# Recommendation tower in float32: six pairs of products a chunk in two parts instead of four, four low parts by VectorE, first transfers and last stage rearranged

## The chip, the core and the metric

The kernel runs on one core of a Trainium2 chip. The metric is the device time of one launch in microseconds (us); lower is better. Engines: TensorE (PE, its weight loads PEld), VectorE (DVE), ScalarE (ACT), GpSimd (POOL), SyncE (SP, which only issues transfers here).

## What is computed

For 512 rows, 32 embeddings of 16 numbers are gathered from 32 tables. Three cross layers follow, each a big matrix product over all products of two fields; then a small dense network.

```python
x0 = h = e                                  # (512, 32, 16)
for i in range(3):
    z = (x0[:, :, None, :] * h[:, None, :, :]).reshape(B, F * G, E)
    y = relu(einsum('oc,bce->boe', Ws[i], z) + bs[i][None, :, None])
    x_keep, h = (y[:, :64], y[:, 64:]) if i != 2 else (y, y)
    xs.append(x_keep)
z = sum(concatenate(xs, axis=1), axis=2)    # (512, 256)
h = maximum(concatenate([z, dense_ctx], 1) @ W_top1 + b_top1, 0)
h = maximum(h @ W_top2 + b_top2, 0)
y = h @ W_top3                              # (512, 1)
```

## The kernel before

**Chunks and steps.** The batch is cut into 16 chunks of 32 rows; a chunk has 32 x 16 = 512 columns. A *step* (layer, chunk, k) makes one group of four product tiles z (128x2048) and multiplies them. Layer 0 has one step a chunk, layers 1 and 2 have four each (k = 0 to 3). A step's four tiles are two *pairs*, i = 0 and 1. The order of steps is a written table. From chunk c = 2 on it repeats, and I number the nine steps of a round s0 to s8:

| s0 | s1 | s2 | s3 | s4 | s5 | s6 | s7 | s8 |
|---|---|---|---|---|---|---|---|---|
| (1,c,0) | (2,c-1,0) | (1,c,1) | (2,c-1,1) | (0,c+1,0) | (1,c,2) | (1,c,3) | (2,c-1,2) | (2,c-1,3) |

**Who does what.** VectorE makes the products z of a step: L414 for layers 1 and 2 (one operand h in PSUM, the other x_pair in SBUF), L402 for layer 0 (both operands in SBUF), and L426 for the squares of layer 0. A pair is multiplied in one of two ways. *Unsplit* (L605): two float32 matmuls, each of which the trace records as two. *Split* (L618): ScalarE rounds z to a high part z_high (L498), another engine subtracts it to get z_low (L362 on GpSimd), and TensorE does six matmuls of the fast rounded type: high by high, high by low weight, low by high weight. The layer 0 split has one more small matmul (L623).

**Order on the engines.** Every engine works through its own list in order. TensorE does at place n of the table first the unsplit pairs of step n and then the split pairs of step n-2 (`BEHIND`). ScalarE does at place n first the layer outputs that are due there (`OUTPUTS`), then the high parts of step n. A layer output (`layer_out`, L512) waits until the last pair of its layer and chunk in TensorE's order (`CLOSES`) is done; then it writes relu of the bank twice, 64 rows each, as h (the input of the next layer's products) and once as kept. The output of (1,c) stands at s8 and that of (0,c+1) at s0 of the next round, in this order. The products of s0 need h of layer 0 (h1), those of s1 need h of layer 1 (h2). Five z slots and four z_high/z_low slots are used in turn.

Before the change, the split pairs of a chunk from 1 on are both pairs of layer 0 and i = 1 of (1,k=0), (1,k=1), (2,k=1) and (2,k=2): six of eighteen, all their low parts on GpSimd. So (1,c) is closed by an unsplit pair of s6.

**Transfers.** GpSimd gathers the embeddings (L349, eight a chunk, three chunks ahead). SyncE stores them to a scratch buffer in DRAM (`store_x`) and loads them back repeated over partitions: `load_x0` (x_rep, x_rot for layer 0, 1.25 MB a chunk) and `load_pair` (x_pair for layers 1 and 2, 4 MB a chunk). At the start TensorE does BUSY = 56 transposes (L658) until the first chunk has arrived.

**Last stage.** The first dense layer's sums go through relu with the bias into hid1, then are rounded and split (L581, L584, L465), and a second dense layer (L628) and the last row (L689, L691) follow.

Of the kernel before, what the change touches and what calls it, by code (L numbers as in the profile page):

```python
# [6 lines left out]
P = 128  # L7
# [3 lines left out]
CHUNKS = BATCH // ROWS  # L11
# [7 lines left out]

Z_SLOTS, PAIR_SLOTS, X_SLOTS = 5, 4, 4  # L20
X0_LOADS, SMALL, TOPS = GROUP + 1, 2, COPIES + 2
BUSY = 56
# [45 lines left out]
FIRST = ([(1, 0, k) for k in range(GROUPS)] + [(2, 0, 0), (0, 1, 0)] + [(2, 0, k) for k in range(1, GROUPS)]  # L68
# [49 lines left out]
def behind():  # L118

    due = {n: [] for n in range(len(PLAN))}  # L120
    for n, step in enumerate(PLAN):
        for pair in step.by("vector", "pool"):
            due[min(n + 2, len(PLAN) - 1)].append(pair)
    return due


BEHIND = behind()
# [17 lines left out]
def dlrm_tower(nc, idx_in, row0_in, ident_in, sel_in, signs_in, columns_in, table, dense, w0_in, w12_in, w_top1, w_top2, out):  # L145
    with ExitStack() as ctx:  # L146
# [6 lines left out]
        def sem(name):  # L153
# [7 lines left out]
        rows_all = sb("rows_all", [P, CHUNKS * GATHERS], I32)  # L161
# [21 lines left out]
        columns = sb("columns", [P, 11])  # L183
        bias, bt1, bt2, wt3 = columns[:, 0:3], columns[:, 3:7], columns[:, 7:9], columns[:, 9:11]
# [23 lines left out]
        hid1 = x_pair[:, 0, 0:4, :]  # L208
# [42 lines left out]
        top1_done, hid1_made, hid1_rounded, hid1_ready = (sem("top1_done"), sem("hid1_made"), sem("hid1_rounded"),  # L251
                                                          sem("hid1_ready"))
# [44 lines left out]
        def _(sp):  # L297
# [37 lines left out]
            tops = [(wd[EMBED * i:EMBED * (i + 1)], w_top1[2 * P:, :]) for i in range(COPIES)] + [  # L335
                (wt1, w_top1[0:2 * P, :].rearrange("(k p) n -> p k n", p=P)),
# [5 lines left out]
            sp.dma_start(out.rearrange("b o -> o b"), result[:]).then_inc(out_stored, 16)  # L342
# [405 lines left out]
```

## Time and profile before

| | |
|---|---|
| median of 3 runs | 548.99 us (548.51 to 549.04) |
| the profiled execution's own time | 548.4 us |
| its span, first to last instruction | 546.6 us |
| TensorE busy | 505.7 us, 93% |
| VectorE busy | 376.5 us, 69% |
| GpSimd busy | 364.1 us, 67% |
| ScalarE busy | 198.8 us, 36% |
| mean granted TensorE clock | 0.978 |

The span is 1.8 us shorter than the execution's own time, which is 0.6 us below the median. A busy share is a mean over stages; which engine sets the time in a round has to be read from the order of events in that round.

### The profile page before, as it was taken

The page shows a single profiled execution, that of the slowest core. Times are in us where ns is not written, and L with a number is a line of the kernel's source. Part 1 is how long each engine was busy: PE and PEld are TensorE (multiplying, and loading weights), DVE is VectorE, ACT ScalarE, POOL GpSimd, SP SyncE. Part 2 cuts the span into 40 slices and gives each one's busy share as a digit, 9 for nine tenths or more (in the row PEclk, how much of TensorE's full clock was granted, in tenths as well). Part 3 has the DMA queues.
Part 4 walks back from the last instruction along what each step waited for, and adds up shares of the span by engine and source line. Part 5 has one row for each costly group of instructions (what it writes and reads, how often), then busy time and mean ns, then how long its engine had stood idle before and what let it go on. Part 6 is the DMA issues. An engine that isn't in the chain of part 4 may idle for free.

```text
span 546.6 us, 4327 instructions
## 1 busy us (share of the span) xinstructions
PE 505.7 (93%) x1474; PEld 277.4 (51%) x1474; DVE 376.5 (69%) x216; ACT 198.8 (36%) x257; POOL 364.1 (67%) x222
## 2 busy tenths in 40 slices
PE   0977947899999999999999999999999989899988
PEld 0733414455555555565555555555555554455555
DVE  1274526595959595959688695959595968967743
ACT  1212132433444443424342434434443525241244
POOL 5770527497969788796969696969697754715050
PEclk9988887899999999999999999999999999999999
DMA  7697989349997979797878787979789777451200
GB/s 229 144 201 204 210 221 196 100 98 252 222 251 170 255 159 254 158 227 166 230 164 226 172 215 165 225 167 244 164 197 222 171 190 161 90 110 11 74 0 0
DMA packets 33591, 94.49 MB, mean 173 GB/s; under 512 B 7889, under 2 KB 15057, under 8 KB 25122
## 3 DMA queue, kind: packets, MB, share of 16 engines
q1 hardware_dynamic: 27090, 90.82, 69.5%
q10 hardware_dynamic: 2384, 2.35, 2.0%
q0 software_dynamic: 4096, 1.06, 1.6%
q8 instruction: 11, 0.18, 0.1%
q14 instruction: 10, 0.08, 0.1%
HBM read 92.04 MB, written 2.10 MB: 172 GB/s over the span
## 4 chain that ended last, share of the span: by engine, by line
PE 73%; DMA 8%; DVE 7%; issue 4%; POOL 3%; SPq 2%; ACT 1%; POOLq 1%; DVEq 0%; ACTq 0%
PE acc L605 26%; PE acc L618 14%; PE spare L605 12%; PE x_bank L605 11%; DMA x_scratch<-gathered 4%; DVE z L414 4%; PE x_bank L618 3%; PE spare L618 3%; POOL gathered L349 3%; DMA gathered<-in_table,rows_all 2%; DMA x_rot<-x_scratch 1%; SPq L276 1%; POOLq L146 1%; DVE zl_parts L426 1%; PE acc L628 1%
## 5 line engine op out<-in xcount | busy, mean ns | idle before, releaser
L362 POOL TENSOR_TENSOR z_low<-z,z_high 128x1024 fp32r<-128x1024 f32 x90 | 221.4, 2472 | 130.1 <-ACT z_high L498 129.4
L414 DVE TENSOR_TENSOR z<-h,x_pair 128x2048 f32<-128x2048 f32 (+1 forms) x65 | 144.8, 2249 | 106.1 <-ACT h L512 104.6
L605 PE MATMUL acc<-z,w_direct 128*128 128x512 f32 x384 | 176.3, 603 | 15.2 <-DVE z L414 15.2
L349 POOL DMA_INDIRECT gathered<-in_table,rows_all x128 | 142.5, 1113 | 33.4 <-issue 27.1
L498 ACT ACTIVATE z_high<-z 128x1024 fp32r<-128x1024 f32 x90 | 93.3, 1054 | 145.1 <-DVE z L414 124.9
L605 PEld LDWEIGHTS acc<-z,w_direct 128*128 128x128 f32 x384 | 73.6, 193 | 95.7 <-issue 72.6
L605 PE MATMUL spare<-z,w_direct 128*128 128x512 f32 x200 | 92.4, 603 | 4.5 <-DVE z L414 4.5
L605 PE MATMUL x_bank<-z,w_direct 128*128 128x512 f32 x200 | 92.5, 608 | 3.9 <-DVE z L414 3.9
L414 DVE TENSOR_TENSOR z<-h_odd,x_pair 128x2048 f32<-128x2048 f32 x32 | 72.2, 2278 | 8.4 <-ACT h_odd L512 8.4
L414 DVE TENSOR_TENSOR z<-h_even,x_pair 128x2048 f32<-128x2048 f32 x32 | 72.2, 2279 | 7.9 <-ACT h_even L512 7.9
L605 PEld LDWEIGHTS spare<-z,w_direct 128*128 128x128 f32 x200 | 38.4, 193 | 47.9 <-issue 43.0
L605 PEld LDWEIGHTS x_bank<-z,w_direct 128*128 128x128 f32 x200 | 38.9, 195 | 45.0 <-issue 43.2
L618 PE MATMUL acc<-z_high,w_high 128*128 128x512 f32 x124 | 57.5, 544 | 1.6 <-POOL z_low L362 1.6
L402 DVE TENSOR_TENSOR z<-x_rep,x_rot 128x2048 f32<-128x2048 f32 x15 | 44.2, 2944 | 7.8 <-DMA x_rot<-x_scratch 7.8
L618 PE MATMUL acc<-z_high,w_low 128*128 128x512 f32 x124 | 38.8, 395 | 0.0
L618 PE MATMUL acc<-z_low,w_high 128*128 128x512 f32 x124 | 38.3, 391 | 0.0
L618 PEld LDWEIGHTS acc<-z_high,w_high 128*128 128x128 f32 x124 | 23.6, 191 | 25.6 <-issue 22.4
L512 ACT ACTIVATE h<-acc,columns 64x512 f32<-64x512 f32 x32 | 20.9, 652 | 39.5 <-PE acc L618 35.2
L512 ACT ACTIVATE kept<-acc,columns 64x512 f32<-64x512 f32 (+1 forms) x32 | 21.9, 683 | 30.4 <-PE acc L618 29.8
L618 PEld LDWEIGHTS acc<-z_low,w_high 128*128 128x128 f32 x124 | 23.3, 188 | 5.4
L618 PEld LDWEIGHTS acc<-z_high,w_low 128*128 128x128 f32 x124 | 23.3, 188 | 5.2
L431 DVE TENSOR_REDUCE sum<-kept 128x32 f32<-128x512 f32 x32 | 21.6, 676 | 5.9 <-ACT kept L512 5.9
(140 smaller groups left out, 266.4 us busy)
## 6 DMA issues: line engine op xcount, KB each, us to landing
x_pair<-x_scratch SPq DMA_DIRECT2D x124, 512.0 KB, 7.3
x_rot<-x_scratch SPq DMA_DIRECT2D x60, 256.0 KB
x_rep<-x_scratch SPq DMA_DIRECT2D x15, 256.0 KB
w_direct<-in_W SPq DMA_DIRECT2D x2, 1024.0 KB, 8.5
gathered<-in_table,rows_all POOLq DMA_INDIRECT x128, 7.1
x_scratch<-gathered SPq DMA_DIRECT2D x32, 64.0 KB, 1.6
x_pair<-x_scratch ACTq DMA_DIRECT2D x4, 512.0 KB, 16.5
x_pair<-in_W_top SPq DMA_DIRECT2D x2, 512.0 KB, 4.7
```

The lines of the kernel that those rows point to most:

```text
L146: with ExitStack() as ctx:
L276: eng.dma_start(x_pair[HALF * a:HALF * (a + 1), c % 2, GROUP * k:GROUP * (k + 1), :], rows.unsqueeze(0).to_broadcast([HALF, GROUP, N])).th ...
L349: pool.indirect_dma_start(gathered[:, c % X_SLOTS, j, :], None, table, bass.IndirectOffsetOnAxis(ap=rows.bitcast(U32), axis=0),).then_inc( ...
L362: nc.gpsimd.tensor_tensor(z_low[:, slot_of(pair)], products_of(pair), z_high[:, slot_of(pair)].bitcast(F32), ALU.subtract).then_inc(low_po ...
L402: nc.vector.tensor_tensor(z[:, step.group % Z_SLOTS], x_rep[:].unsqueeze(1).to_broadcast([P, GROUP, N]), x_rot[:], ALU.mult).then_inc(z_ma ...
L414: nc.vector.tensor_tensor(z[:, step.group % Z_SLOTS, first:end], h[:].unsqueeze(1).to_broadcast([P, end - first, N]), x_pair[:, chunk % 2, ...
L426: nc.vector.scalar_tensor_tensor(out=zl_parts[:], in0=zl_high[:].bitcast(F32), scalar=signs[:, 0:1], in1=zl_full[:], op0=ALU.mult, op1=ALU ...
L431: nc.vector.tensor_reduce(total[:, chunk * ROWS:(chunk + 1) * ROWS], kept.rearrange("p (b e) -> p b e", b=ROWS), AX.X, ALU.add).then_inc(m ...
L498: nc.scalar.activation(z_high[:, slot_of(pair)], products_of(pair), ACT.Copy).then_inc(high_made, 1)
L512: return nc.scalar.activation(dst, bank[rows, :], ACT.Relu, bias=bias[rows, layer:layer + 1])
L605: op = nc.tensor.matmul(bank_of(pair)[:], w_direct[:, first + i], products_of(pair)[:, i], start=i == 0 and pair is OPENS[pair.layer, pair ...
L618: op = nc.tensor.matmul(bank_of(pair)[:], w[:, at + i], zs[:, slot, i], start=part == i == 0 and pair is OPENS[pair.layer, pair.chunk], st ...
```

## The change

It has four parts. (1) `SPLIT` gets two more entries, (1,2,1) and (2,0,1): eight of a chunk's eighteen pairs are split. (2) Four of the low parts, (0,0,1), (1,2,1), (2,0,1) and (2,1,1), and all of layer 2 in the last chunk, go to VectorE, one place behind their products (`LOWS`). (3) The first transfers are issued in another order, the steps (2,0,1) and (0,1,0) change places, the products of (2,0,0) come in two halves, and BUSY is 28. (4) In the last stage the bias of the first dense layer is a row of the dense matmul, so one ScalarE operation makes the rounded hid1 straight from the bank, VectorE makes its low part from the bank, and TensorE begins each k with the four matmuls that need only the high part.

```diff
-BUSY = 56
+BUSY = 28
-FIRST = ([(1, 0, k) for k in range(GROUPS)] + [(2, 0, 0), (0, 1, 0)] + [(2, 0, k) for k in range(1, GROUPS)]
+FIRST = ([(1, 0, k) for k in range(GROUPS)] + [(2, 0, 0), (2, 0, 1), (0, 1, 0), (2, 0, 2), (2, 0, 3)]
-SPLIT = ((1, 0, 1), (1, 1, 1), (2, 1, 1), (2, 2, 1))
+SPLIT = ((1, 0, 1), (1, 1, 1), (1, 2, 1), (2, 0, 1), (2, 1, 1), (2, 2, 1))
+BY_VECTOR = ((0, 0, 1), (1, 2, 1), (2, 0, 1), (2, 1, 1))
 def hands(layer, chunk, k):
-    return tuple("pool" if chunk and (layer, k, i) in AT else "tensor" for i in range(2))
+    def by(of):
+        if not chunk or of not in AT:
+            return "tensor"
+        return "vector" if of in BY_VECTOR or (layer, chunk) == (2, CHUNKS - 1) else "pool"
+
+    return tuple(by((layer, k, i)) for i in range(2))
...
+def lows():
+
+    due = {n: [] for n in range(len(PLAN))}
+    for n, step in enumerate(PLAN):
+        for pair in step.by("vector"):
+            due[min(n + 1, len(PLAN) - 1)].append(pair)
+    return due
...
             sp.wait_ge(x_stored[0], 32)
-            for k in range(GROUPS):
+            for k in range(2):
                 load_half(sp, 0, k, 0)
             store_x(sp, 1)
+            for k in range(2, GROUPS):
+                load_pair(0, k)
             sp.wait_ge(start_done, 1)
             load_x0(sp, 1)
-            for k in range(GROUPS):
+            store_x(sp, 2)
+            for k in range(2):
                 load_pair(1, k)
+            wait_made(sp, STEPS[0, 1, 0])
+            sp.wait_ge(last_made, 2)
+            load_x0(sp, 2)
+            for k in range(2, GROUPS):
+                load_pair(1, k)
...
                 free_slot(step)
                 (products if step.layer else products0)(step)
-                for pair in BEHIND[n]:
-                    if pair.by == "vector":
-                        low_part(pair)
+                for pair in LOWS[n]:
+                    low_part(pair)
...
                 act.wait_ge(top1_done, m + 1)
-                nc.scalar.activation(hid1[:, m, :], top_bank[m][:], ACT.Relu,
-                                     bias=bt1[:, m:m + 1]).then_inc(hid1_made, 1)
-                act.wait_ge(hid1_made, m + 1)
-                nc.scalar.activation(hid1_high[:, m, :], hid1[:, m, :], ACT.Copy).then_inc(hid1_rounded, 1)
+                nc.scalar.activation(hid1_high[:, m, :], top_bank[m][:], ACT.Relu).then_inc(hid1_rounded, 1)
```

`BEHIND`, `OUTPUTS`, the order of the nine steps and the number of slots stay (only the split pairs of (0,1) come one place earlier). How the order changes on three engines is shown at one place each, the middle of the program.

TensorE before, from the split pairs of s4 (which close layer 0 of the next chunk in acc0) to s0 of the next round:

```order
L618 MATMUL acc0<-z_high,w_high 128x512 [waits low_pool]
L618 MATMUL acc0<-z_high,w_high 128x512
L623 MATMUL acc0<-zl_parts,wl_parts 128x512 [waits last_parts]
L618 MATMUL acc0<-z_high,w_low 128x512 x2
L618 MATMUL acc0<-z_low,w_high 128x512 x2
L605 MATMUL x_bank<-z,w_direct 128x512 [waits z_made]
L605 MATMUL x_bank<-z,w_direct 128x512
L605 MATMUL x_bank<-z,w_direct 128x512 [waits z_made]
L605 MATMUL x_bank<-z,w_direct 128x512
```

TensorE now, at the same place (spare is the bank of layer 1):

```order
L645 MATMUL acc0<-z_low,w_high 128x512 x2
L632 MATMUL acc2<-z,w_direct 128x512 [waits z_made]
L632 MATMUL acc2<-z,w_direct 128x512
L645 MATMUL spare<-z_high,w_high 128x512 [waits low_dve]
L645 MATMUL spare<-z_high,w_high 128x512
L645 MATMUL spare<-z_high,w_low 128x512 x2
L645 MATMUL spare<-z_low,w_high 128x512 x2
L632 MATMUL acc2<-z,w_direct 128x512 [waits z_made]
L632 MATMUL acc2<-z,w_direct 128x512
```

Behind the close of layer 0 there now stand the unsplit pair of s7 and then the split pair of s5, which is the last of layer 1: (1,c) closes two pairs after (0,c+1), where it used to close before it.

ScalarE at the end of a round, before (first fence) and now (second): the output of layer 1, then that of layer 0.

```order
L512 ACTIVATE h2_even<-spare,columns 64x512 [waits z_made,direct_used]
L512 ACTIVATE h2_even<-spare,columns 64x512
L512 ACTIVATE kept01<-spare,columns 64x512
L512 ACTIVATE h1<-acc0,columns 64x512 [waits sum01_made,z_made,pairs_used]
```

```order
L542 ACTIVATE h2_even<-spare,columns 64x512 [waits z_made,pairs_used]
L542 ACTIVATE h2_even<-spare,columns 64x512
L542 ACTIVATE kept01<-spare,columns 64x512
L542 ACTIVATE h1<-acc0,columns 64x512 [waits sum01_made,z_made,pairs_used]
```

The order is the same; h2 now waits for a split pair (`pairs_used`), and h1 stands behind it.

VectorE, the products from s2 to s6 before:

```order
L414 TENSOR_TENSOR z<-h1,x_pair 128x2048 [waits xp_here_0_1,direct_used]
L431 TENSOR_REDUCE sum01<-kept01 128x32 [waits kept1_out]
L414 TENSOR_TENSOR z<-h2_odd,x_pair 128x2048 [waits low_pool,direct_used]
L431 TENSOR_REDUCE sum2<-kept2 128x32 [waits kept2_out]
L402 TENSOR_TENSOR z<-x_rep,x_rot 128x2048 [waits x0_here,direct_used]
L426 SCALAR_TENSOR_TENSOR zl_parts<-zl_high,signs,zl_full 128x512 [waits last_high]
L414 TENSOR_TENSOR z<-h1,x_pair 128x2048 [waits xp_here_0_2,low_pool,direct_used]
L414 TENSOR_TENSOR z<-h1,x_pair 128x2048 [waits xp_here_0_3,low_pool,direct_used]
```

and now:

```order
L442 TENSOR_TENSOR z<-h1,x_pair 128x2048 [waits xp_here_0_1,direct_used]
L449 TENSOR_TENSOR z_low<-z,z_high 128x1024 [waits high_made]
L459 TENSOR_REDUCE sum01<-kept01 128x32 [waits kept1_out]
L442 TENSOR_TENSOR z<-h2_odd,x_pair 128x2048 [waits low_pool,direct_used]
L459 TENSOR_REDUCE sum2<-kept2 128x32 [waits kept2_out]
L430 TENSOR_TENSOR z<-x_rep,x_rot 128x2048 [waits x0_here,direct_used]
L449 TENSOR_TENSOR z_low<-z,z_high 128x1024 [waits high_made]
L454 SCALAR_TENSOR_TENSOR zl_parts<-zl_high,signs,zl_full 128x512 [waits last_high]
L442 TENSOR_TENSOR z<-h1,x_pair 128x2048 [waits xp_here_0_2,low_pool,direct_used]
L449 TENSOR_TENSOR z_low<-z,z_high 128x1024 [waits high_made]
L442 TENSOR_TENSOR z<-h1,x_pair 128x2048 [waits xp_here_0_3,low_dve,direct_used]
```

Three low parts (L449) stand ahead of the products of s6, and a fourth right behind them.

## Rows read from the trace of the kernel before

**Rows 1.** The page: span; busy time, share and instructions of each engine.

```profile
span 546.6 us, 4327 instructions
PE 505.7 (93%) x1474; PEld 277.4 (51%) x1474; DVE 376.5 (69%) x216; ACT 198.8 (36%) x257; POOL 364.1 (67%) x222
```

**Rows 2.** The chain that ended last, one round: start us, us, what.

```profile
245.18 6.87 PE acc L605 x16
252.04 1.37 PE acc L618 x6
...
256.85 1.72 PE acc L605 x4
...
271.31 1.85 PE acc L618 x8
274.30 5.15 PE x_bank L605 x12
```

**Rows 3.** Timeline at a round's end: start us, us, engine, line, what [idle before].

```profile
271.35 1.32 ACT L512 ACTIVATE h_odd<-acc,columns 64x512 f32<-64x512 f32 x2 [3.32 <-PE acc L605]
...
272.69 0.68 ACT L512 ACTIVATE kept<-acc,columns 64x512 f32<-64x512 f32 x1
...
274.34 1.32 ACT L512 ACTIVATE h<-acc,columns 64x512 f32<-64x512 f32 x2 [0.97 <-PE acc L618]
...
275.79 2.29 DVE L414 TENSOR_TENSOR z<-h,x_pair 128x2048 f32<-128x2048 f32 x1 [6.65 <-ACT h L512]
```

```profile
274.14 5.31 PE L605 MATMUL x_bank<-z,w_direct 128*128 128x512 f32 x12
```

**Rows 4.** Timeline of the round without gathers, by engine (VectorE, GpSimd, TensorE).

```profile
430.81 0.68 DVE L431 TENSOR_REDUCE sum<-kept 128x32 f32<-128x512 f32 x1
431.40 3.03 DVE L402 TENSOR_TENSOR z<-x_rep,x_rot 128x2048 f32<-128x2048 f32 x1
434.36 2.86 DVE L426 SCALAR_TENSOR_TENSOR zl_parts<-zl_high,signs,zl_full 128x512 fp32r<-128x512 f32 x1
437.15 4.48 DVE L414 TENSOR_TENSOR z<-h,x_pair 128x2048 f32<-128x2048 f32 x2
```

```profile
429.92 11.85 POOL L362 TENSOR_TENSOR z_low<-z,z_high 128x1024 fp32r<-128x1024 f32 x4 [2.67 <-ACT z_high L498]
```

```profile
439.48 3.70 PE L605 MATMUL acc<-z,w_direct 128*128 128x512 f32 x8 [1.66 <-DVE z L414]
```

**Rows 5.** Groups by line and shape: busy us, mean ns | idle before.

```profile
L362 POOL TENSOR_TENSOR z_low<-z,z_high 128x1024 fp32r<-128x1024 f32 x90 | 221.4, 2472 | 130.1 <-ACT z_high L498 129.4
...
L498 ACT ACTIVATE z_high<-z 128x1024 fp32r<-128x1024 f32 x90 | 93.3, 1054 | 145.1 <-DVE z L414 124.9 <-DVE z L402 20.2
...
L465 DVE TENSOR_TENSOR z_low<-x_pair,z_high 128x1024 fp32r<-128x1024 f32 x1 | 1.2, 1207 | 0.0
```

**Rows 6.** TensorE behind a gap: its timeline, then the 2 us window after it (granted clock ahead of the last two figures).

```profile
105.83 5.40 PE L605 MATMUL acc<-z,w_direct 128*128 128x512 f32 x8 [2.14 <-DVE z L414]
```

```profile
106.00:108.00 2.00, 2.00 (x3) 0.81 (x4) 2.00 (x2) 0.00 (x0) 1.70 (x2) 0.53 0.12 16
```

**Rows 7.** Timeline of the head.

```profile
13.93 7.96 PE L658 MATMUL acc<-ident 128*128 128x128 f32 x56
...
80.58 2.29 DVE L402 TENSOR_TENSOR z<-x_rep,x_rot 128x2048 f32<-128x2048 f32 x1 [7.83 <-DMA x_rot<-x_scratch]
...
98.66 2.29 DVE L414 TENSOR_TENSOR z<-h,x_pair 128x2048 f32<-128x2048 f32 x1 [7.94 <-ACT h L512]
```

```profile
85.79 3.59 PE L605 MATMUL acc<-z,w_direct 128*128 128x512 f32 x4 [11.00 <-DVE z L414]
```

**Rows 8.** Timeline of the last chunk and the last stage.

```profile
483.45 2.29 DVE L414 TENSOR_TENSOR z<-h,x_pair 128x2048 f32<-128x2048 f32 x1 [6.43 <-ACT h L512]
...
529.47 0.52 PE L670 MATMUL h<-dense_parts,wd_parts 48*128 48x512 f32 x1
...
536.57 0.47 PE L628 MATMUL acc<-z_high,w_high 128*128 128x512 f32 x1 [0.23 <-DVE z_low L465]
```

More of the change, by code:

```diff
@@ L122, in behind @@
         for pair in step.by("vector", "pool"):
-            due[min(n + 2, len(PLAN) - 1)].append(pair)
+            due[min(n + (1 if (pair.layer, pair.chunk) == (0, 1) else 2), len(PLAN) - 1)].append(pair)
     return due
-BEHIND = behind()
+def lows():
[4 more added lines that the diff above has]
+    return due
+BEHIND, LOWS = behind(), lows()
+HALVED = (STEPS[1, 0, 0], STEPS[2, 0, 0])
 ORDER = list(START.pairs)
@@ L132 @@
 CLOSES = {(pair.layer, pair.chunk): pair for pair in ORDER}
-LAST1 = max((pair for step in PLAN for pair in step.by("pool") if step.layer < 2), key=lambda pair: pair.split)
-LAST_SLOT = max((pair for step in PLAN for pair in step.by("pool") if pair.split % PAIR_SLOTS == PAIR_SLOTS - 1),
+LAST1 = max((pair for step in PLAN for pair in step.by("vector", "pool") if step.layer < 2),
+            key=lambda pair: pair.split)
+LAST_SLOT = max((pair for step in PLAN for pair in step.by("vector", "pool") if pair.split % PAIR_SLOTS == 0),
                 key=lambda pair: pair.split)
@@ L411, in products @@
                 h = h1 if step.layer == 1 else h2[chunk % 2]
-                runs = ((0, 2), (2, 4)) if step is PLAN[0] else ((0, 4),)
+                runs = ((0, 2), (2, 4)) if step in HALVED else ((0, 4),)
                 for first, end in runs:
@@ L543, in _ @@
             act.wait_ge(dense_turned, 1)
-            nc.scalar.activation(dense_high[:], dense_bank[0:COPIES * EMBED, :], ACT.Copy).then_inc(dense_rounded, 1)
+            nc.scalar.activation(dense_high[:], dense_bank[0:COPIES * DENSE, :], ACT.Copy).then_inc(dense_rounded, 1)
             act.wait_ge(x_stored[0], 32)
-            for k in range(GROUPS):
+            for k in range(2):
                 load_half(act, 0, k, 1)
@@ L598, in unsplit @@
                     pe.wait_ge(w12_here[pair.layer - 1], 16)
-                if step is PLAN[0] and pair.i == 0:
-                    pe.wait_ge(first_made, 1)
+                if step in HALVED and pair.i == 0:
+                    pe.wait_ge(first_made, HALVED.index(step) + 1)
                 else:
@@ L679, in _ @@
             for k in range(4):
+                pe.wait_ge(hid1_rounded, k + 1)
+                for m in range(2):
+                    cols = slice(k * 2 * P + m * P, k * 2 * P + (m + 1) * P)
+                    nc.tensor.matmul(acc[m][:], wt2_high[:, cols], hid1_high[:, k, :], start=k == 0, stop=False)
+                    nc.tensor.matmul(acc[m][:], wt2_low[:, cols], hid1_high[:, k, :], start=False, stop=False)
                 pe.wait_ge(hid1_ready, k + 1)
                 for m in range(2):
[L682 to L684 removed]
+                    cols = slice(k * 2 * P + m * P, k * 2 * P + (m + 1) * P)
+                    op = nc.tensor.matmul(acc[m][:], wt2_high[:, cols], hid1_low[:, k, :], start=False, stop=k == 3)
                     if k == 3:
@@ L719 @@
         "table": np.concatenate(tables, axis=0),
-        "dense_ctx": np.asarray(inputs["dense_ctx"]),
+        "dense": np.concatenate([np.asarray(inputs["dense_ctx"]), np.ones((BATCH, 1), np.float32)], axis=1),
     }
```

76 lines of the change are left out of this document (38 added, 38 removed).

## The prediction, written before the changed kernel ran

> **What bounds the kernel now.** I read the page first: TensorE is busy for 505.7 of 546.6 us, VectorE for 376.5 [rows 1]. Then the chain that ended last. From about 110 us to 420 us it is TensorE and nothing else: in [rows 2] the reader sees one of ten equal rounds, from 245.18 to 274.30 us, 29.1 us each. An unsplit pair takes 1.72 us (x4), a split pair 1.37 to 1.39 (x6), and the two pairs of layer 0 with their extra matmul 2.99 (271.31 to 274.30). Twelve unsplit pairs, four split ones and this block give 20.6 + 5.5 + 3.0 = 29.1: no gap is in it.
>
> Then I asked how near the other engines come to ending last, at a round's end and in its middle. At the end [rows 3]: TensorE begins the next work at 274.14, so layer 0 has closed; ScalarE writes h1 from 274.34 for 1.32 us, VectorE starts the products of s0 at 275.79, that is 1.65 us after the close, and needs 2.29. They end at 278.1; TensorE has three pairs meanwhile, 5.15 us, to 279.3, so h1 comes 1.2 us ahead of need. VectorE had waited 6.65 us, but this wait is no free time: it stands behind h1, so whatever is added to VectorE's list ahead of s6 comes after it. So there is a second chain round the loop: close of layer 0, h1, VectorE's products s0 to s6, the two pairs of s6, the split pairs of s4, close of the next layer 0. How little air it has is shown where gathers end and four low parts of GpSimd come in a row [rows 4]: L402 takes 3.03 and L426 2.86 us, because VectorE's operations with both operands in SBUF and GpSimd's subtraction exclude each other (GpSimd's four need 11.85 us, where four of the mean 2.47 of [rows 5] are 9.9). That is 2.1 us more on VectorE, and TensorE stands for 1.66 us at 439.48, at s6.
>
> **The change, part by part.**
>
> *TensorE's work.* Two more split pairs a chunk save 2 x (1.72 - 1.38) = 0.67 us a round: 28.45 us of work instead of 29.12. This would be the gain, if TensorE stayed the bound.
>
> *VectorE's new work.* A low part with 128x1024 elements took 1.21 us on VectorE [rows 5]; starts of successive operations lie 0.08 us closer than their durations, so I take 1.13 each. It needs the high part, 1.06 us on ScalarE [rows 5], which begins 0.1 us after the products. I walk one round from the start of the products of s0 (0), with products 2.20 apart (from 4.48 for two), sums 0.60 (430.81 to 431.40), squares 0.66 (0.74 less the overlap) [rows 4]. Products s1 at 2.20, s2 at 4.40. The low part of s1 could start at 6.60, but its high part stands on ScalarE behind kept of layer 2, which waits for TensorE to close that layer behind s0: 2.33 + 1.72 + 1.38 = 5.43; kept 5.63, high part 6.22 to 7.28; low part 7.32. Sum 8.45, products s3 9.04, sum 11.24, products s4 11.84, low part of s3 14.04, squares 15.17, products s5 15.83, low part of s4 18.03, where GpSimd is still at its own low part of s4 until 18.3, so 0.25 later than free; products s6 19.41, done at 21.69. TensorE by then has done s0 to s5 with gaps of 1.1 us ahead of s3 and 2.3 us ahead of s5 and waits 0.5 us for s6. It then does the pairs of s6 (3.43) and of s4 (2.99).
>
> *The close of layer 1.* In this kernel the split pair of s5 is layer 1's last. TensorE reaches it two pairs after the close of layer 0: 1.72 + 1.38 = 3.10 us later, at 21.73 + 3.43 + 2.99 + 3.10 = 31.25. ScalarE has the output of layer 1 in its list ahead of h1. So h1 waits for a close that it doesn't need: 0.20 to start, 1.34 for h2, 0.68 for kept, 1.32 for h1, 0.13 to VectorE [rows 3] make 3.67. The products of the next s0 start at **34.9**. TensorE has only s8 to cover this, 3.43 us against 3.67 + 2.33, so it stands for 2.5 us there. The new round is 34.9 us against 29.1, +5.8. Without the late close it would be 31.25 - 3.10 + 1.65 = 29.8: the low parts alone cost 0.7 a round, the close 5.1. Queued behind the waiting h1 are all products of the round; behind VectorE's wait for the high part of s1 are s3 to s8.
>
> *Gaps and TensorE's clock.* The walk assumes full clock. In the trace a gap of 2.14 us is followed by a stretch at about half (0.53 granted, the lower level, 1.2 GHz), in which eight matmuls take 5.40 us instead of 3.60: 1.8 us lost [rows 6]. The gap of 1.66 us cost nothing: 3.70 [rows 4]. Shown as the profile shows them (0.15 less than from start to start), the gaps of the walk are 2.35 us ahead of s0 and 2.15 ahead of s5. A loss behind s0 delays the close of layer 2 and so the low part of s1: up to 1.8 a round. A loss behind s5 has 0.5 us of air: up to 1.3. So 0 to 3.1 a round. Both gaps are at or a little above the one that fell, one case only, so I take the middle, 1.5.
> The Trainium skill's page "TensorE: Matmul & The Clock Gate", section "HAM oscillation — how this bites in real kernels", warns of idle gaps longer than any in this walk; by that rule the clock would stay up and nothing be added, and the trace's 2.14 us gap disagrees with it.
>
> *Head.* 28 fewer transposes of 0.142 us [rows 7] start the first chunk 4.0 us earlier; halving the products of (2,0,0) lets TensorE start 1.1 sooner. VectorE's wait of 7.83 us for x_rot ahead of (0,2,0) goes, since this load is now issued one layer 0 step earlier, ahead of two of the four x_pair loads. So TensorE's start at 85.79 [rows 7] comes at 72.9. From there to the products of s0 of chunk 2 there were 12.9 us; now two unsplit pairs, one split and the block, 3.44 + 1.38 + 2.99 = 7.8, a stretch at half clock as now (1.8) and 1.65: 84.1 instead of 98.66, -14.5. Bounds: -4 (only the warm-up) and -18. But layer 1 of chunk 1 then closes 7.9 us after layer 0 and h2 holds up s1 by 5.7 us; with the wait for kept gone (0.7), the first round is 39.9.
>
> *The other rounds.* From s0 of chunk 3 to s0 of chunk 15 there are 12 rounds: 418.8. So s0 of chunk 15 starts at 84.1 + 39.9 + 418.8 = 542.8 (now 483.45 [rows 8]). From there to TensorE's first dense matmul there are 46.0 us (to 529.47). The same walk without a layer 0 step gives 48.0, since the high parts of the last layer 2 pairs wait for the output of chunk 14 and VectorE carries them all; 49 with a half loss of clock.
>
> *Last stage.* 17.1 us from there to the end. TensorE is busy all through it but for 0.23 us at 536.57 [rows 8], which the shorter hand-over removes: -0.3. The removed ScalarE operations (four of 0.7) lie under TensorE's work of the first dense layer.
>
> *Sum.* 542.8 + 49 + 17.1 - 0.3 = 608.6 at full clock, and 13 rounds x 1.5 = 20 for the clock: a span of 628.6, +82 on 546.6. The median lies 2.4 us above the span: **631 us**.
>
> **Rivals.**
> *The clock stays up* in all rounds: 608.6 + 2.4 = 611. For it: the gap of 1.66 that cost nothing, and gaps that are only just longer than the one that did. Against it: that one.
> *The clock falls behind both gaps in every round:* 608.6 + 40 + 2.4 = 651.
> *The other side: h1 isn't held up,* the close of layer 1 coming in time. The place is ScalarE's wait at s8. If the round is 29.8, the 13 rounds give back 66 us of the 82: 608.6 - 66 + 2.4 = 545, and with TensorE as the only bound (28.45 a round) 527. It decides as soon as ScalarE serves h1 within 1.65 us of the close. Against it: the lists of both engines stand fixed, h2 ahead of h1, and the split pair of s5 two pairs after the close. Nothing in the trace lets ScalarE pass a wait.
> *The gather or the loads become late:* a longer round gives them more time; no price.
>
> **How the numbers follow.** Clock falls in part of the gaps: 0.5. Stays up: 0.25. Falls always: 0.18. Not held up: 0.04. Something outside: 0.03. The range goes from a little below the second to the third, with -4 for the head (-18 instead of -14.5): 606 to 652. A difference below 0.2% (1.1 us) can't be told from none here. Slower by more than that holds 0.95; faster 0.04; the same 0.01.
>
> **What would show it.** In the changed profile: rounds of 35 to 38 us in place of 29.1; "DVE z <- ACT h" still the longest wait of VectorE, and TensorE idle <- DVE z in every round, at s0 (2.4 us), s3 (1 us) and s5 (2 us), with VectorE's low part at 1.2 us; ScalarE's h2 starting 0.2 us after a split pair, h1 2.0 us behind it; the granted clock at its lower level in some slices all through the middle; GpSimd's wait for high parts grown. The prediction is wrong if the rounds stay near 29 us, which would mean that h1 is served ahead, or if VectorE's operations are each longer than in these rows.

## The result, and the profile after

The changed kernel took 653.36 us (median of 4 runs, 651.42 to 654.54) against 548.75 us (548.32 to 549.04) for the kernel before on the same chip: a ratio of 1.1925, 95% interval [1.1896, 1.1954]. Predicted were 631 us, 606 to 652. The direction and the mechanism came as forecast; the time lies 22 us above the forecast and 1.4 outside the range. The page of the changed kernel (span, busy time, and in slices TensorE's busy tenths and its granted clock):

```profile
span 651.3 us, 4498 instructions
PE 538.7 (83%) x1506; PEld 296.9 (46%) x1506; DVE 436.6 (67%) x280; ACT 227.1 (35%) x285; POOL 309.1 (47%) x191
PE   1877697978888897888889888888889788889978
PEclk9989997988889998889999888988988898899989
```

Against [rows 1], TensorE is no longer the bound (83%, and part of its busy time is a slower clock), VectorE is 60 us busier, GpSimd 55 us less. The digits 8 of the clock row run all through the middle.

One round, read as [rows 3, 4] were. VectorE (start us, us, what, and idle time before it with what ended it):

```profile
318.93 2.29 DVE L442 TENSOR_TENSOR z<-h,x_pair 128x2048 f32<-128x2048 f32 x1 [7.82 <-ACT h L542]
...
328.04 1.23 DVE L449 TENSOR_TENSOR z_low<-z,z_high 128x1024 fp32r<-128x1024 f32 x1 [2.42 <-ACT z_high L528]
...
334.76 1.22 DVE L449 TENSOR_TENSOR z_low<-z,z_high 128x1024 fp32r<-128x1024 f32 x1
...
338.76 1.21 DVE L449 TENSOR_TENSOR z_low<-z,z_high 128x1024 fp32r<-128x1024 f32 x1
...
356.99 2.29 DVE L442 TENSOR_TENSOR z<-h,x_pair 128x2048 f32<-128x2048 f32 x1 [9.28 <-ACT h L542]
```

ScalarE at this round's end:

```profile
353.50 1.32 ACT L542 ACTIVATE h_even<-spare,columns 64x512 f32<-64x512 f32 x2 [6.90 <-PE spare L645]
354.84 0.68 ACT L542 ACTIVATE kept<-spare,columns 64x512 f32<-64x512 f32 x1
355.54 1.31 ACT L542 ACTIVATE h<-acc,columns 64x512 f32<-64x512 f32 x2
```

TensorE's three gaps in it:

```profile
321.37 2.59 PE L632 MATMUL spare<-z,w_direct 128*128 128x512 f32 x4 [2.54 <-DVE z L442]
...
332.11 1.98 PE L632 MATMUL acc<-z,w_direct 128*128 128x512 f32 x4 [0.95 <-DVE z L442]
...
338.90 3.11 PE L632 MATMUL spare<-z,w_direct 128*128 128x512 f32 x4 [2.06 <-DVE z L442]
```

And windows of 2 us (granted clock ahead of the last two figures), two behind the first gap and one behind the third:

```profile
322.00:324.00 2.00, 2.00 (x5) 0.84 (x4) 2.00 (x2) 0.31 (x1) 1.61 (x1) 0.64 0.23 66
324.00:326.00 2.00, 2.00 (x6) 1.52 (x6) 1.62 (x1) 0.00 (x0) 1.71 (x2) 0.51 0.79 188
...
340.00:342.00 2.00, 2.00 (x4) 0.87 (x3) 2.00 (x1) 0.00 (x0) 1.70 (x2) 0.50 1.05 381
```

The reader sees the chain of the prediction step by step: the output of layer 1 (h_even, at 353.50) ahead of h (355.54), VectorE's products 1.45 us behind that, its whole list behind them, and TensorE idle at s0, s3 and s5. New is how often the clock falls: behind the gap at s0 in every round, behind that at s5 in eight rounds of twelve. The eight rounds with both falls are 38.1 us long and the four with one are 36.7; the mean of the twelve, from s0 of chunk 3 to s0 of chunk 15, is 37.61.

The head on VectorE, for [rows 7], and the first products of chunk 2:

```profile
40.10 2.29 DVE L442 TENSOR_TENSOR z<-h,x_pair 128x2048 f32<-128x2048 f32 x1 [6.08 <-DMA x_pair<-x_scratch]
45.15 2.29 DVE L442 TENSOR_TENSOR z<-h,x_pair 128x2048 f32<-128x2048 f32 x1 [2.76 <-DMA x_pair<-x_scratch]
...
91.67 2.29 DVE L442 TENSOR_TENSOR z<-h,x_pair 128x2048 f32<-128x2048 f32 x1 [2.83 <-ACT h L542]
```

and TensorE's transposes at the start, with the first matmul behind them:

```profile
14.23 5.44 PE L685 MATMUL acc<-ident 128*128 128x128 f32 x28
19.60 1.12 PE L662 MATMUL x_bank<-x_rot 32*128 32x512 f32 x2
```

The last chunk's s0 and the first dense matmul, for [rows 8]:

```profile
582.64 2.29 DVE L442 TENSOR_TENSOR z<-h,x_pair 128x2048 f32<-128x2048 f32 x1 [9.28 <-ACT h L542]
```

```profile
634.27 0.50 PE L697 MATMUL h<-dense_parts,wd_parts 51*128 51x512 f32 x1
```

### The profile page after: what moved, and what is told of

Read it like the earlier page. It is cut to its first block, busy times and chain, and to the rows that moved or that the text cites. A ratio compares the mean times of both kernels' runs of the same rounds, so it can differ in the third digit from the quotient of the medians.

```text
span 651.3 us, 4498 instructions
## 1 busy us (share of the span) xinstructions
PE 538.7 (83%) x1506; PEld 296.9 (46%) x1506; DVE 436.6 (67%) x280; ACT 227.1 (35%) x285; POOL 309.1 (47%) x191
## 4 chain that ended last, share of the span: by engine, by line
PE 49%; DVE 28%; issue 10%; ACT 7%; DMA 3%; POOL 2%; SPq 0%; DVEq 0%; ACTq 0%
DVE z L442 17%; PE acc L632 15%; PE acc L645 13%; PE spare L632 11%; DVE z L430 4%; PE x_bank L645 4%; DVE z_low L449 3%; ACT h L542 3%; DVE sum L459 3%; PE x_bank L632 3%; ACT z_high L528 2%; POOL gathered L377 2%; PE spare L645 2%; DVE zl_parts L454 1%; ACT kept L542 1%
## 5 line engine op out<-in xcount | busy, mean ns | idle before, releaser
L390 POOL TENSOR_TENSOR z_low<-z,z_high 128x1024 fp32r<-128x1024 f32 x59 | 147.9, 2507 | 264.5 <-ACT z_high L528 264.4
L528 ACT ACTIVATE z_high<-z 128x1024 fp32r<-128x1024 f32 x120 | 123.7, 1054 | 200.7 <-DVE z L442 182.8
L377 POOL DMA_INDIRECT gathered<-in_table,row x128 | 161.0, 1258 | 34.9 <-issue 27.5
L632 PEld LDWEIGHTS acc<-z,w_direct 128*128 128x128 f32 x320 | 62.7, 203 | 122.2 <-issue 79.0
L449 DVE TENSOR_TENSOR z_low<-z,z_high 128x1024 fp32r<-128x1024 f32 x61 | 76.2, 1249 | 34.9 <-ACT z_high L528 34.9
L632 PE MATMUL x_bank<-z,w_direct 128*128 128x512 f32 x172 | 79.7, 597 | 11.3 <-DVE z L442 11.3
L645 PE MATMUL acc<-z_high,w_high 128*128 128x512 f32 x156 | 78.2, 584 | 0.0
L442 DVE TENSOR_TENSOR z<-h_even,x_pair 128x2048 f32<-128x2048 f32 (+1 forms) x33 | 72.4, 2216 | 5.3 <-ACT h_even L542 5.3
L645 PE MATMUL acc<-z_high,w_low 128*128 128x512 f32 x156 | 49.9, 401 | 0.0
L542 ACT ACTIVATE h_even<-spare,columns 64x512 f32<-64x512 f32 x16 | 10.4, 652 | 66.7 <-PE spare L645 45.3
```

The source lines that it names most:

```text
L377: pool.indirect_dma_start(gathered[:, c % X_SLOTS, j, :], None, table, bass.IndirectOffsetOnAxis(ap=rows.bitcast(U32), axis=0),).then_inc( ...
L390: nc.gpsimd.tensor_tensor(z_low[:, slot_of(pair)], products_of(pair), z_high[:, slot_of(pair)].bitcast(F32), ALU.subtract).then_inc(low_po ...
L442: nc.vector.tensor_tensor(z[:, step.group % Z_SLOTS, first:end], h[:].unsqueeze(1).to_broadcast([P, end - first, N]), x_pair[:, chunk % 2, ...
L449: nc.vector.tensor_tensor(z_low[:, slot_of(pair)], products_of(pair), z_high[:, slot_of(pair)].bitcast(F32), ALU.subtract).then_inc(low_dv ...
L528: nc.scalar.activation(z_high[:, slot_of(pair)], products_of(pair), ACT.Copy).then_inc(high_made, 1)
L542: return nc.scalar.activation(dst, bank[rows, :], ACT.Relu, bias=bias[rows, layer:layer + 1])
```

## The experiments

A round below is the time from one s0 of VectorE (its products with h of layer 1) to the next. The prediction's walk gave 34.9 us for it at full clock; before it was 29.13 (31.0 in the last two). Diffs are against the changed kernel unless another is named.

### The rounds: what is late, and what the clock costs

**e1, h1 served ahead of h2.** Layer 1's output goes into ScalarE's list one step later.

```
-    at |= {(1, c): PLACE[2, c - 1, GROUPS - 1] if c >= 2 else PLACE[2, c, 0] for c in range(CHUNKS)}
+    at |= {(1, c): PLACE[1, c + 1, 0] if 2 <= c < CHUNKS - 1 else PLACE[2, c - 1, GROUPS - 1] if c >= 2
+           else PLACE[2, c, 0] for c in range(CHUNKS)}
```

> The changed kernel, with ScalarE's output of layer 1 moved behind that of layer 0 (from s8 to s0 of the next round, h1 ahead of h2). Theory (the close of layer 1 holds up h1): s0's products start 1.65 us behind the close of layer 0, not 6.8; the gap ahead of s0 goes. What ends last then is the low part of s1, whose high part stands behind kept of layer 2: walk 32.2 us a round, 33 with the clock falling behind s5. 653 - 13 x (37.6 - 32.2 to 33) = 583 to 594. Rival (VectorE's four low parts are the cost, wherever h1 stands): rounds above 36 us, over 630.

Measured: 596.77 us (one run; the kernel before took 549.16 on this chip), span 595.0, rounds of 32.22 and 33.6 us, 33.16 in the mean. So h2's place ahead of h1 costs 4.45 us a round, and the twelve rounds give back 53 of the 105 us. The time lies 3 us above the expectation: the clock fell behind s5 in eight of the twelve rounds, which makes them 33.6. At full clock the place costs 34.9 less 32.2, 2.7 and not the 5.1 that the prediction had put on it. The timeline of this kernel shows where the rest stays (VectorE's s0, ScalarE's output of layer 2, VectorE's first low part):

```profile
292.89 2.29 DVE L443 TENSOR_TENSOR z<-h,x_pair 128x2048 f32<-128x2048 f32 x1 [4.09 <-ACT h L543]
...
301.08 0.69 ACT L543 ACTIVATE kept<-x_bank,columns 128x512 f32<-128x512 f32 x1 [3.43 <-PE x_bank L646]
...
302.75 1.23 DVE L450 TENSOR_TENSOR z_low<-z,z_high 128x1024 fp32r<-128x1024 f32 x1 [2.26 <-ACT z_high L529]
```

ScalarE writes layer 2's output 8.19 us behind s0 instead of the prediction's 5.63: when h1 comes early, TensorE still has the pairs of s7, s5 and s8 before it (1.72 + 1.38 + 3.43), so it enters s0 later relative to VectorE. The low part of s1, behind that close in ScalarE's list, moves from 7.32 to 9.86, and with it everything behind. What the early h1 gains at one end, the close of layer 2 takes back in part.

**e2, all low parts on GpSimd.**

```
-BY_VECTOR = ((0, 0, 1), (1, 2, 1), (2, 0, 1), (2, 1, 1))
+BY_VECTOR = ()
```

> The changed kernel with all low parts on GpSimd (eight split pairs a chunk as before it); the last chunk's layer 2 stays with VectorE. Theory (late close): h1 is still held up, TensorE's gap of 2.4 us ahead of s0 stays and with it the fall of the clock; 3.67 + 2.33 + 15.5 (TensorE's work s0 to s5) + 6.42 + 3.10 = 31.0 us a round, up to 33 with the clock: 567 to 595. Rival (VectorE's new work is the whole cost): rounds near 29, about 545. Third (GpSimd becomes the bound: eight low parts of 2.5 and eight gathers of 1.25 make 30): idle TensorE waits for z_low, not for z.

Measured: 616.62 us (one run), most rounds of 33.76 or 35.1, mean 34.62: 3.0 less than in the changed kernel, but 22 us above the expectation. The rounds of 33.76 are those in which the clock stayed up; against the 34.93 of e3 below, which is the changed kernel's round at full clock, the four low parts on VectorE cost 1.2 us, and the rest of the 3.0 is the clock's. GpSimd's and TensorE's timeline, at the moment that the split pair of s2 is due:

```profile
316.61 3.05 POOL L377 DMA_INDIRECT gathered<-in_table,row  x1
...
319.68 2.37 POOL L390 TENSOR_TENSOR z_low<-z,z_high 128x1024 fp32r<-128x1024 f32 x1
...
322.11 0.73 PE L645 MATMUL spare<-z_high,w_high 128*128 128x512 f32 x2 [1.86 <-POOL z_low L390]
```

A gather that issues in 0.95 us elsewhere took 3.05 while VectorE worked at its layer 0 products (316.55, both operands in SBUF); the low part behind it comes late, and TensorE now waits for GpSimd where it had waited for VectorE.

The same round shows something on the clock: the gap at s0 is as long as in the changed kernel, and the four matmuls behind it run at full clock (1.96 us where they took 2.59; granted clock 1.00 in the window of 2 us behind it).

```profile
309.00 1.96 PE L632 MATMUL spare<-z,w_direct 128*128 128x512 f32 x4 [2.54 <-DVE z L442]
```

```profile
310.00:312.00 2.00, 2.00 (x9) 1.31 (x8) 2.00 (x2) 0.00 (x0) 1.98 (x1) 1.00 0.00 0
```

**e3, the clock held up.** Fifteen transposes of the identity into a bank that the next pair opens fill TensorE's gaps at s0 and s5. They compute nothing.

```
+                if step.chunk >= 2 and pair.i == 0 and (pair.layer, pair.k) in ((1, 0), (1, 2)):
...
+                    for _ in range(FILL):
+                        nc.tensor.transpose(bank[:, 0:P], ident[:], ident[:])
```

> The changed kernel with 15 transposes of 0.14 us ahead of TensorE's s0 and s5 from chunk 2 on, into banks that are free there (2.1 us of work in gaps of 2.5 and 2.2); nothing else differs. Theory (the gaps cost clock, 2.7 of the 37.6 us a round): granted clock at its upper level in the middle, rounds of 34.9 us, 653 - 35 = 618. Rival (the rounds are longer than the walk for another reason, a queue or the shared port): rounds stay at 37 to 38, 650 or more.

Measured: 624.74 us (one run), 28.6 less than the changed kernel. The page's clock row and TensorE's timeline:

```profile
PEclk9979978999999999999999999999999999999989
```

```profile
309.37 1.80 PE L634 MATMUL spare<-ident 128*128 128x128 f32 x15
311.98 1.98 PE L641 MATMUL spare<-z,w_direct 128*128 128x512 f32 x4 [0.81 <-DVE z L443]
...
325.68 1.80 PE L634 MATMUL acc<-ident 128*128 128x128 f32 x15
327.91 1.98 PE L641 MATMUL spare<-z,w_direct 128*128 128x512 f32 x4 [0.43 <-DVE z L443]
```

The same gaps are there, only filled; the four matmuls behind them take 1.98 us where they took 2.59 and 3.11. Every round in the middle is 34.93 us: the walk, to 0.03. So the walk was right, and 37.61 - 34.93 = 2.7 us a round are the clock's. The twelve rounds give back 32 us; the head was 1.3 and the first round 2.3 longer, in the latter the filling also stands in TensorE's way.

**e6, the late close alone, and e5 as its base.** e5 keeps the changed head and last stage but has the four split pairs of the kernel before, all low parts on GpSimd. e6 only exchanges (2, 2, 1) for (1, 2, 1), the split pair that closes layer 1 late. (In both, the last stage also uses other z_high and z_low slots than the changed kernel.)

```
e5:
-SPLIT = ((1, 0, 1), (1, 1, 1), (1, 2, 1), (2, 0, 1), (2, 1, 1), (2, 2, 1))
+SPLIT = ((1, 0, 1), (1, 1, 1), (2, 1, 1), (2, 2, 1))
-        return "vector" if of in BY_VECTOR or (layer, chunk) == (2, CHUNKS - 1) else "pool"
+        return "pool"
e6 against e5:
+SPLIT = ((1, 0, 1), (1, 1, 1), (1, 2, 1), (2, 1, 1))
```

> The changed kernel with the four split pairs of the kernel before, all low parts on GpSimd: only the first transfers, BUSY 28, the halves and the last stage are changed. The head gave 7.0 us in the changed kernel (s0 of chunk 2 at 91.67 instead of 98.66), the last stage should give 0.3, rounds stay at 29.1: 548.8 - 7.3 = 541.5. Rival (the head's gain was part of the other rounds' change and is given back where layer 1 of chunk 1 closes): 546 to 549.

> As e5, but the fourth split pair is (1,2,1) instead of (2,2,1): as much work for TensorE and GpSimd, none for VectorE, only layer 1 now closes behind layer 0. Theory (the late close alone lengthens the loop): s0's products 6.8 us behind the close of layer 0, + 18.1 + 6.42 = 31.3 a round, 31.8 with the clock; 13 x (31.3 to 31.8 less 29.1) = 29 to 35 above e5, 571 to 577. Rival (it costs only together with VectorE's low parts, which fill the slack): no slower than e5 by more than 5 us.

Measured: e5 562.84 us, ratio 0.9884 [0.981, 0.9958] to the kernel before, which took 567.45 here; e6 625.49, ratio 1.1007 [1.0916, 1.1098]. (On the chips of e5 to e12 the first chunk was late: VectorE's first products with x_rep started at 37 to 48 us in these eight traces, at 21.69 in the changed kernel's. The kernel before left no trace there, but took 18 us more than elsewhere. So these times stand only beside each other, and e5's and e9's miss of the expected 541 to 543 tells nothing of the head.) Rounds are 29.13 in e5 and 33.77 in e6: one split pair in another place, with no work added, costs 4.6 us a round. ScalarE, VectorE and TensorE in e6, and TensorE one round later:

```profile
318.88 1.32 ACT L542 ACTIVATE h_odd<-acc,columns 64x512 f32<-64x512 f32 x2 [13.40 <-PE acc L645]
...
320.92 1.31 ACT L542 ACTIVATE h<-acc,columns 64x512 f32<-64x512 f32 x2
...
322.37 2.29 DVE L442 TENSOR_TENSOR z<-h,x_pair 128x2048 f32<-128x2048 f32 x1 [11.60 <-ACT h L542]
324.81 1.77 PE L632 MATMUL spare<-z,w_direct 128*128 128x512 f32 x3 [2.54 <-DVE z L442]
...
358.56 1.96 PE L632 MATMUL acc<-z,w_direct 128*128 128x512 f32 x4 [2.54 <-DVE z L442]
```

The expectation was 2 us a round too low. 1.7 of it is another unsplit pair that lies ahead of the late one in this kernel. The clock has no part in it: it fell behind the gap of 2.54 in the first of these rounds and not in the next, and both are 33.8 us long; where it did not fall, TensorE waits 1.1 us more at a later place. The rest was not taken apart.

**e4, h1 first and only two low parts on VectorE; e8, with the output of layer 2 later as well.** Candidates to beat both kernels with six split pairs. e8 also has the loads of e7 below.

```
e4, besides the edit of e1:
-BY_VECTOR = ((0, 0, 1), (1, 2, 1), (2, 0, 1), (2, 1, 1))
+BY_VECTOR = ((1, 2, 1), (2, 2, 1))
e8, besides:
-    at |= {(2, c): PLACE[2, c + 1, 0] if c else PLACE[1, 1, 1] for c in range(CHUNKS - 1)}
+    at |= {(2, c): PLACE[2, c + 1, 0] + 1 if c else PLACE[1, 1, 1] for c in range(CHUNKS - 1)}
```

> Eight split pairs, h1 ahead of h2 as in e1, and VectorE's low parts only those of s5 and s7, which come behind its products of s6; GpSimd has the six ahead of them. Theory (what counts is what stands between h1 and s6 on VectorE): the loop is 27 us and TensorE is the bound with 28.45 a round: 548.8 - 13 x 0.67 - 7 (head) = 533, at most 540. Rival (eight split pairs can't be fed): rounds of 30 us or more, above 550.

> e4 with kept of layer 2 one step later on ScalarE, behind the high part of s1, and the loads of e7. In e4 TensorE stood 2.3 us a round for GpSimd's low part of s1, whose high part waited for kept. Theory (that order is what is left): rounds at TensorE's work, 28.5 us; e7 less 12 x 0.67 = 529. Rival (GpSimd, with six low parts and eight gathers and the shared port held by VectorE's two more low parts, is the next bound): rounds of 29.5 to 31 us, 545 to 565, TensorE waiting for z_low.

Measured: e4 571.19 us (one run), rounds 31.27, clock 0.982; e8 581.85, ratio 1.026 [1.0176, 1.0343], rounds 30.6 in the middle. Both expectations missed, and the rounds are those of the rivals. In e4 TensorE waits 1.65 us a round for a low part of GpSimd. In e8 it waits 1.9 us for VectorE's products and not for GpSimd; VectorE has no wait left in the middle (none from 240 to 340 us), and its own operations are long:

```profile
279.96 5.04 DVE L429 TENSOR_TENSOR z<-x_rep,x_rot 128x2048 f32<-128x2048 f32 x1
280.46 2.38 POOL L389 TENSOR_TENSOR z_low<-z,z_high 128x1024 fp32r<-128x1024 f32 x1
...
289.35 4.70 POOL L389 TENSOR_TENSOR z_low<-z,z_high 128x1024 fp32r<-128x1024 f32 x2
289.98 5.16 DVE L448 TENSOR_TENSOR z_low<-z,z_high 128x1024 fp32r<-128x1024 f32 x1
```

Alone these take 2.28 and 1.21 us; the mean of its 32 low parts is 2.58. Both operations begin while GpSimd is at a gather or a low part, and end only 2.2 and 1.1 us behind the end of the low part that follows it (282.84 and 294.05). The Trainium skill's page "SBUF — State Buffer", section "SBUF: two separate sides", calls the pair of ports that VectorE and GpSimd share an exclusive lock, held for the whole instruction; the runs agree, with 5.04 in place of 2.28. Which engine gets in first is not shown: in [rows 4] the two took turns, here GpSimd went twice.

**e11, five split pairs, and e12, the price of low parts on VectorE.** Both against e9 (the kernel of e5 again): e11 splits (2, 0, 1) too and has the later output of layer 2 of e8 (two edits at once), all low parts on GpSimd; e12 moves two of the six low parts to VectorE (four stay on GpSimd).

```
e11:
+SPLIT = ((1, 0, 1), (1, 1, 1), (2, 0, 1), (2, 1, 1), (2, 2, 1))
e12:
+BY_VECTOR = ((0, 0, 1), (2, 1, 1))
```

> The changed kernel with the four split pairs of the kernel before and all low parts on GpSimd, so only the head and the end of the program are changed; the same kernel as e5, on another chip I hope, since there the first chunk of every kernel was some 20 us late. By the changed kernel's trace the head is worth 7.0 us (s0 of chunk 2 at 91.67 in place of 98.66) and the end 1 or less; rounds of 29.13. So 541 to 543 against 549. By the prediction's step for the head (14.5) it would be 534.

> A candidate to beat both: e9 with the second pair of (2,c-1,0) split as a fifth, its low part and all others on GpSimd, the output of layer 2 in ScalarE's list one step later, and no split pair that closes layer 1 late. If TensorE stays the bound, a round is 28.8 (0.34 less than 29.13) and 13 rounds give 4.4 us: 537 to 538. Rival: GpSimd's two low parts of s0 and s1 in a row hold the port that it shares with VectorE, VectorE's products and so h1's cover of 1.2 us go, and rounds are 29.5 to 31: 546 to 566.

> The price of low parts on VectorE by itself: e9 with the low parts of layer 0's second pair and of (2,c-1,1) on VectorE (1.13 us each from start to start), the two others on GpSimd. No late close and no more split pairs. Theory: VectorE is 2.3 us longer ahead of s6, but its operations no longer wait 2 us for the port, and h1 came 1.2 us ahead of need: rounds of 29.1 to 29.4, within 4 us of e9. Rival: a low part on VectorE costs its full time on the path from h1 to s6, as these stand ahead of it: rounds of 30.2, 14 us above e9.

Measured on one chip (the kernel before: 566.61): e9 565.75 us, ratio 0.9958 [0.9925, 0.9991]; e11 585.03, 1.0283 [1.0226, 1.0341]; e12 573.65, 1.01 [1.0064, 1.0136]. Rounds 29.13, 30.90 and 30.06. One split pair more with its low part on GpSimd, and the later output, cost 1.8 us a round instead of saving 0.3; the layer 0 products take 5.02 us in the timeline, 4.21 in the mean of all chunks, where the kernel before has 2.94:

```profile
317.61 5.02 DVE L430 TENSOR_TENSOR z<-x_rep,x_rot 128x2048 f32<-128x2048 f32 x1
318.08 2.39 POOL L390 TENSOR_TENSOR z_low<-z,z_high 128x1024 fp32r<-128x1024 f32 x1
320.63 2.83 POOL L377 DMA_INDIRECT gathered<-in_table,row  x1 [0.16 <-issue]
```

Two low parts on VectorE cost 0.93 us a round, between my theory (0 to 0.3) and the rival (1.1).

### The head: the loads behind the store

**e7, e10, e14: the loads of chunk 0's x_pair all ahead of the store of chunk 1,** on the kernel of e5 (which is also e9 and e13), on three chips. **e15** is the same edit in the changed kernel itself.

```
-            for k in range(2):
+            for k in range(GROUPS):
                 load_half(sp, 0, k, 0)
             store_x(sp, 1)
-            for k in range(2, GROUPS):
-                load_pair(0, k)
...
             act.wait_ge(x_stored[0], 32)
-            for k in range(2):
+            for k in range(GROUPS):
                 load_half(act, 0, k, 1)
```

The changed kernel had not only put the loads of k = 2 and 3 behind that store, it had also given them whole to SyncE. The edit undoes both: ScalarE issues the second half of each again. These runs do not tell the two apart.

> As e5, but all eight x_pair halves of chunk 0 are issued ahead of the store of chunk 1, as in the kernel before. Theory (the changed head lost 5 us of its expected 14.5 where VectorE waited 6.1 and 2.8 us for the x_pair loads of k = 2 and 3, which stand behind that store): these waits shrink to 0 to 1.3 us and the first h2 comes 4 to 5 us earlier: 537, 4 to 5 below e5. Rival (the store and the loads of chunk 1 then come later by as much, and x_rot of chunk 2 is waited for again): e5 within 1 us or slower.

> e9 with all loads of the first chunk's x_pair ahead of the store of chunk 1 (the kernel e7). If the prediction missed the head because two of the four loads now stand behind that store (waits of 6.08 and 2.76 us against 0.24 and 1.26), this gives 4 to 7 us back on e9: 535 to 538. If the head is held by something else (the wait for x_rot, the later loads of chunk 1), it equals e9.

> The kernel of e5 and e9 a third time, for a chip whose first chunk is not late: the first s0 of chunk 2 at 91.7 as in the changed kernel, waits for x_pair of some 6 and 3 us, rounds of 29.13, and 541 to 543 against 549. By the prediction's step for the head it would be 534.

> The kernel of e7 and e10 on the same chip. If the two x_pair loads that were put behind the store of chunk 1 hold the head, their waits are back at 0.2 and 1.3 us and it ends 4 to 7 us ahead of e13: 535 to 538. If the first chunk is late again (waits for x_rep of 20 us and more), nothing is told and it equals e13.

> The changed kernel itself with these loads ahead of the store of chunk 1, all else unchanged. If the loads are the head's missed 7.6 us, its s0 of chunk 2 starts at 84 to 88 in place of 91.67 and the rounds stay at 36.7 and 38.1: 646 to 649. If the spread (later by 1.7 us) or the load of x_rot holds the head, 650 to 653.

Measured: e7 563.32 us (ratio 0.9928 [0.9892, 0.9964]) against e5's 562.84, and e10 564.77 (0.9955 [0.9921, 0.9989]) against e9's 565.75: against e5 and e9 that tells nothing, since the late first chunk lies ahead of the first use of these loads and can hide them. On the third chip, where the first chunk is not late (the kernel before 547.77): e13 543.90, ratio 0.9924 [0.9888, 0.996]; e14 538.56, ratio 0.9818 [0.9785, 0.9852]. VectorE's waits for x_pair, first in e13, then in e14:

```profile
40.05 2.29 DVE L442 TENSOR_TENSOR z<-h,x_pair 128x2048 f32<-128x2048 f32 x1 [6.65 <-DMA x_pair<-x_scratch]
45.35 2.29 DVE L442 TENSOR_TENSOR z<-h,x_pair 128x2048 f32<-128x2048 f32 x1 [3.01 <-DMA x_pair<-x_scratch]
```

```profile
35.74 2.29 DVE L440 TENSOR_TENSOR z<-h,x_pair 128x2048 f32<-128x2048 f32 x1 [1.22 <-DMA x_pair<-x_scratch]
40.04 2.29 DVE L440 TENSOR_TENSOR z<-h,x_pair 128x2048 f32<-128x2048 f32 x1 [2.01 <-DMA x_pair<-x_scratch]
```

The fourth product comes 5.3 us earlier, s0 of chunk 2 5.2 (89.61 after 94.83), the end 5.3. e13 also shows that the changed head and last stage by themselves bring 3.9 us and not the expected 6 to 8; its s0 of chunk 2 starts 3.2 us later than in the changed kernel, which was not followed up. In e15 (645.82 us, one run) s0 of chunk 2 starts at 87.23, 4.4 us ahead of the changed kernel; its span is 7.3 shorter because one round besides (126.88 to 161.90, 35.0 us) kept its clock behind both gaps. e14 is the best version found, 1.8% ahead of the kernel before: the changed head and last stage with the old split and the old place of the loads.

## Why the prediction was right and wrong

In spans it was 651.3 measured less 628.6 predicted, 22.7 us. By the prediction's own steps:

**The walk of a round: right.** 34.9 predicted, 34.93 in e3, and its gaps (2.35, 1.1, 2.15) measured at 2.54, 0.95 and 2.06. That the late close holds up h1 and with it VectorE's whole list is shown by e1 (4.45 us a round back) and e6 (4.6 lost by one moved pair).

**"So I take the middle, 1.5" for the clock: the step that failed.** It fell behind the gap at s0 every time, and behind that at s5 two times of three: 2.7 us a round, shown by e3. Twelve rounds x 1.2 are 14.5 of the 22.7 us; the first round came 1.7 shorter than the 41.4 of the sum. The price of one fall was right: 1.75 us at s0 (36.68 less 34.93) and 1.39 at s5 (38.07 less 36.68), for 1.8 and 1.3. Wrong was how often it falls, and one row of a gap (2.14 us) could not tell that: the same gap of 2.14 was followed by a fall in e13 and not in e14, and gaps of 2.54 at s0 by a fall in 13 of 13 cases here, 5 of 13 in e2 and 6 of 13 in e6. What decides it is open. The third rival, 651 at a chance of 0.18, came nearest, but in part by luck: the clock cost less than its 40 us, and the head lost 7.6 that it did not have. By the rule on idle gaps that the prediction weighed there, from the Trainium skill's page "TensorE: Matmul & The Clock Gate", section "HAM oscillation — how this bites in real kernels", nothing would have been added; these runs disagree with it at 2.06 and at 2.54 us.

**The head, -14.5: half of it came.** s0 of chunk 2 started at 91.67, not 84.1: +7.6. "28 fewer transposes of 0.142 us" was 5.44 us for 28 where 56 had taken 7.96, so 2.5 saved instead of 4.0 (the first ones are the slow ones: in the trace of the kernel before they start 0.21 us apart up to 17.35 us and 0.11 us apart from there). The larger part is that the loads of k = 2 and 3 were put behind the store of chunk 1 and given to SyncE alone; I had counted what the reordering brings at x_rot and not what comes later by it at x_pair. e14 against e13 shows 5.2 us for that at s0 of chunk 2, e15 against the changed kernel 4.4. Together that is 6 to 7 of the 7.6; the rest stays open.

**The end: +2.8.** From s0 of chunk 15 to the first dense matmul 51.6 us and not 49, then 17.0 and not 16.8. In the windows of this stretch the granted clock is at 0.50 twice, at 586 to 588 us and at 624 to 626; the sum had half a loss there. But the first of the two cost nothing: in e3 it did not happen, and the same way takes 51.7 us. The second is in both, behind a gap of 4.06 us that the walk did not have. How the 2.6 are made up stays open.

7.6 + 14.5 - 1.7 + 2.8 = 23.2, and 0.5 less for the 20 us that the sum had rounded up from 19.5: 22.7.

**"The low parts alone cost 0.7 a round, the close 5.1": right in the sum, wrong as two prices.** With h1 served first the round is 32.2, not 29.8. The step left out was TensorE's backlog: VectorE starts s0 sooner, TensorE doesn't, so the close of layer 2 comes 2.56 us later behind s0 and ScalarE's list passes this on to the first low part. At full clock the close is worth 2.7, and 3.1 belong to the extra low parts and the order around them (two of them alone 0.93, e12). With the close late, e2 gives 1.2 for all four low parts (34.93 less 33.76). This changed nothing of the forecast, but e2, e4 and e8 missed in the same manner: each took away one wait and met the next. The rival "h1 isn't held up", priced at 545 from rounds of 29.8, would have been some 31 us too cheap (13 rounds x 2.4).

**The saving of 0.67 us of TensorE work a round** came nowhere, as forecast: no variant with more than four split pairs besides those of layer 0 went below 30.6.

## What to carry to other kernels

Before moving work between engines to save time on the busiest one, follow the loop from a layer's close to the next start through every list that is fixed in order; here one pair in another place cost 4.6 us a round (e6) and two low parts on VectorE 0.9 (e12). Where a loop has more than one wait, their prices don't add: walk the loop again with the one removed. And where a reordering of transfers brings one forward, list what it puts back, and look up its next consumer in the timeline.

## What the runs showed of the hardware

In the changed kernel TensorE's granted clock fell behind idle gaps of 2.54 us in every round and behind gaps of 2.04 to 2.08 in two of three (the 36.7 us rounds are those where it did not). The length of the gap alone does not decide it: behind gaps of 2.54 it stayed up in 8 of 13 cases in e2 and 7 of 13 in e6. Behind the shorter ones, 1.65 us in all ten rounds of e4 and 0.43 to 0.97 everywhere, it stayed up. Filling the gaps with 1.80 us of transposes that compute nothing kept it up in every round, so a gap that can't be closed can be made cheap, 28.6 us in all here.

On the ports that VectorE and GpSimd share, the layer 0 products, 2.28 us alone, took 3.03 where they got in behind the low part that was running [rows 4], and 5.02 to 5.04 where GpSimd began one more low part first. A gather's issue went from 0.95 to 2.83 and 3.05 us beside them.
